# Last two groups of pass 1 joined in a seven-product scheme, first loads split, and a new order of matmuls in pass 2

## What is computed

```python
base = jnp.einsum('bsi,oi->bso', x, W)                       # W 512 x 512
low = jnp.einsum('bsi,bir->bsr', x, lora_A[labeler_index])   # rank 32, 5 labels
delta = jnp.einsum('bsr,or->bso', low, lora_B_w) * 0.5
x = x + base + delta
```

```python
K = 2.0 * jnp.einsum('hn,hnl->hl', Ct, jnp.exp(P)).real      # 32 heads x 512 taps
y = irfft(rfft(x, n=1024) * rfft(K, n=1024)[None])[..., :512] + x * D[:, None]
x = x + y * (arange(512) < length)[:, None, :]
```

## Time and profile before

| | us |
|---|---|
| three timed runs | 192.64, 192.66, 196.02; median 192.66 |
| the profiled execution, its own time | 192.58 |
| its span, first to last instruction | 190.9 |
| TensorE busy | 185.6 (97%) |
| VectorE, ScalarE, GpSimd busy | 125.9, 91.3, 68.7 |
| group 5 of pass 1 with the taps | about 81.4 to 97.5 |
| groups 6 and 7 | about 97.5 to 126.6 |
| pass 2 | about 126.6 to 187.9 |

### The profile page before, as it was taken

The page is one execution under the profiler, slowest core; times in us unless marked ns, Lnnn a source line. Parts: engine busy times, 40 slices in busy tenths (PEclk is TensorE's granted clock), DMA queues, the critical chain, the costliest instruction groups (busy, mean ns, idle before and its releaser), DMA issues.

```text
span 190.9 us, 2653 instructions
## 1 busy us (share of the span) xinstructions
PE 185.6 (97%) x933; PEld 156.6 (82%) x933; DVE 125.9 (66%) x164; ACT 91.3 (48%) x144; POOL 68.7 (36%) x111
## 2 busy tenths in 40 slices
PE   7799999999999999999999999999999999999994
PEld 2487887888888888888888888888999999999993
DVE  0599979458977048858607407279987777786743
ACT  2456066254148754154463312766565656565600
POOL 6038840000000268100000000379886666676600
PEclk9999999999999999999999999999999999999999
DMA  6999990000000000000001600045988788897433
GB/s 191 349 366 422 424 408 11 0 0 2 3 2 0 0 2 3 0 0 0 0 3 34 200 0 0 0 146 167 309 285 295 282 261 291 277 274 270 181 139 138
DMA packets 14797, 27.35 MB, mean 143 GB/s; under 512 B 2592, under 2 KB 5056, under 8 KB 13888
## 3 DMA queue, kind: packets, MB, share of 16 engines
q1 hardware_dynamic: 14064, 25.81, 39.1%
q10 hardware_dynamic: 720, 1.38, 2.1%
HBM read 18.71 MB, written 8.47 MB: 142 GB/s over the span
## 4 chain that ended last, share of the span: by engine, by line
PE 95%; DVE 2%; ACT 1%; issue 0%
PE y_ps L553 13%; PE y_ps L554 12%; PE y_ps L555 12%; PE k_ps L620 10%; PE k_ps L621 10%; PE k_ps L622 10%; PE low_ps L547 4%; PE low_ps L549 4%; PE low_ps L548 4%; PE y_ps L560 4%; PE y_ps L569 2%; PE y_ps L573 2%; PE y_ps L577 2%; PE low_ps L526 2%; PE k_ps L536 1%; PE k_ps L555 1%
## 5 line engine op out<-in xcount | busy, mean ns | idle before, releaser
L406 POOL TENSOR_TENSOR t_lo<-w_raw,t_hi 128x512 fp32r<-128x512 f32 x32 | 44.3, 1393 | 38.0 <-ACT t_hi L468 37.8
L620 PE MATMUL k_ps<-xs_hi,t_hi 128*128 128x128 f32 (+3 forms) x130 | 41.5, 319 | 0.2 <-DVE x_all L829 0.2
L621 PE MATMUL k_ps<-xs_hi,t_lo 128*128 128x128 f32 (+3 forms) x130 | 41.5, 319 | 0.0
L622 PE MATMUL k_ps<-xs_lo,t_hi 128*128 128x128 f32 (+3 forms) x130 | 41.4, 318 | 0.0
L553 PE MATMUL y_ps<-x_hi,w_hi 128*128 128x512 f32 x104 | 40.6, 391 | 0.0
L555 PE MATMUL y_ps<-x_lo,w_hi 128*128 128x512 f32 x104 | 40.6, 391 | 0.0
L554 PE MATMUL y_ps<-x_hi,w_lo 128*128 128x512 f32 x104 | 40.6, 390 | 0.0
L757 DVE COPY_PREDICATED low_sel<-lab_mask,low_ps 32x512 f32<-32x512 int32 x32 | 23.3, 729 | 25.0 <-PE low_ps L549 24.1
L829 DVE COPY_PREDICATED x_all<-len_mask,k_ps 128x512 f32<-128x512 int32 x31 | 23.3, 750 | 13.1 <-PE k_ps L622 13.0
L769 DVE TENSOR_TENSOR xs_lo<-x_all,xs_hi 128x512 fp32r<-128x512 f32 x32 | 28.1, 883 | 4.6 <-ACT xs_hi L462 4.6
L462 ACT CAST xs_hi<-x_all 128x512 fp32r<-128x512 f32 x32 | 19.9, 622 | 19.7 <-PE k_ps L622 19.7
(11 more groups left out here) (132 smaller groups left out, 221.4 us busy)
## 6 DMA issues: line engine op xcount, KB each, us to landing
w_raw<-k_pad SPq DMA_DIRECT2D x32, 256.0 KB, 4.2
out<-x_all SPq DMA_DIRECT2D x31, 256.0 KB, 3.3
x_all<-in_xt SPq DMA_DIRECT2D x7, 1024.0 KB, 12.3
w_raw<-in_wt ACTq DMA_DIRECT2D x4, 256.0 KB, 5.4
x_all<-in_xt SPq DMA_DIRECT2D x4, 256.0 KB, 7.2
ab_raw<-in_ab SPq DMA_DIRECT2D x1, 320.0 KB, 3.7
...
```

The source lines that it names most:

```text
L406: g.tensor_tensor(t_lo[:, k % TR, :], t_raw[:, k % RAW, ::-1], f32(t_hi[:, k % TR, :]), ALU.subtract).then_inc(t_lo_done, 1)
L620: mm(o, t_hi[:, u, cols(lag)], xs_hi[:, b, x], start=(lag == 0), stop=False, skip_group_check=True)
L621: mm(o, t_lo[:, u, cols(lag)], xs_hi[:, b, x], start=False, stop=False, skip_group_check=True)
L622: return mm(o, t_hi[:, u, cols(lag)], xs_lo[:, b, x], start=False, stop=ends, skip_group_check=True)
```

## The change

**Groups 6 and 7 together** (`PAIR` = 6). The two groups' x (8 heads) and W are seen as 2 x 2 blocks, and the four block products with their sums are made with seven products instead of eight (Strassen's scheme in its form with fifteen sums). GpSimd makes the four sums of W's quarters (in place in `w_raw`) and four of the x quarters (in place in `x_all`) after `k_gains`, and then three `_lo` parts of the W sums; ACT and DVE split the seven x operands; the remaining seven sums are taken on DVE and ACT when products leave PSUM (`mix`, DVE; `alpha_read`, ACT). The low-rank part of group 7 is made from the sum of A's halves, and one B difference is needed. Each product is 12 matmuls of 512 columns.

**The first loads.** `ab_raw` comes in two transfers, its first 32 rows first, and the cast of the first `x_hi` moves from ACT to DVE.

**Pass 2.** In `pass2` the three lag-3 matmuls (128 columns) no longer stand together at the head's end, but one behind each of the three lag-0 matmuls (512 columns). The empty table `BETWEEN` and its code are gone. SBUF buffers are laid out anew; `t_raw` loads wait for the last W sum's `_lo`.

On POOL, after `k_gains`:

```diff
+            pool.wait_ge(w_hi_done, CH + 1)
+            pool.wait_ge(w_lo_done, CH)
...
+            g.tensor_tensor(w22, w21, w22, ALU.add).then_inc(s_sum, 1)
+            pool.wait_ge(s_sum, 1)
+            g.tensor_tensor(w21, w21, w11, ALU.subtract).then_inc(s_sum, 1)
+            pool.wait_ge(s_sum, 2)
+            g.tensor_tensor(w11, w22, w11, ALU.subtract).then_inc(s_sum, 1)
+            pool.wait_ge(s_sum, 3)
+            g.tensor_tensor(w12, w12, w11, ALU.subtract).then_inc(s_sum, 1)
...
+            pool.wait_ge(x_load[PAIR], 16)
+            pool.wait_ge(op_lo_done, op_at["X11"])
+            g.tensor_tensor(x11, x12, x11, ALU.subtract).then_inc(x_sum, 1)
+            pool.wait_ge(x_sum, sum_at["T1"])
+            g.tensor_tensor(x12, x12, x22, ALU.subtract).then_inc(x_sum, 1)
+            pool.wait_ge(x_sum, sum_at["T3"])
+            pool.wait_ge(op_lo_done, op_at["X22"])
+            g.tensor_tensor(x22, x22, x11, ALU.subtract).then_inc(x_sum, 1)
+            pool.wait_ge(x_sum, sum_at["T2"])
+            pool.wait_ge(op_lo_done, op_at["X21"])
+            g.tensor_tensor(x21, x21, x22, ALU.subtract).then_inc(x_sum, 1)
```

On ACT, in the loop over g, ahead of `stack_low(g)`:

```diff
+                if g == ACT_KGEN:
+                    act.wait_ge(x_load[PAIR - 1], 16)
+                    split_op_hi("X11")
+                    act.wait_ge(x_load[PAIR], 16)
+                    split_op_hi("X22")
...
+                if g == PAIR - 1:
+
+                    act.wait_ge(x_used, PAIR - 1)
+                    act.wait_ge(x_sum, sum_at["T3"])
+                    split_op_hi("T3")
+                    act.wait_ge(x_sum, sum_at["T2"])
+                    split_op_hi("T2")
```

On DVE, in the loop over g and behind it:

```diff
                 if g == DVE_KGEN:
                     k_reciprocal()
+                    split_op_lo("X11")
+                    split_op_lo("X22")
                 if g == DVE_KGEN + 1:
                     k_scale()
+                    split_op_lo("X21")
...
+                if g == PAIR - 1:
+                    split_op_lo("T3")
+                    split_op_lo("T2")
+
+            split_op_lo("T4")
+            split_op_lo("T1")
+            select_low(PAIR)
+            select_low(PAIR + 1)
+
+            def mix(d, o, i, bank, m):
+                dve.wait_ge(m_done, m_at[m] + d + 1)
+                v.tensor_tensor(o, i, bank[d].rearrange("p (h b) -> p h b", b=P), ALU.add).then_inc(mixed, 1)
```

On PE, a product, and the third of the seven, behind group 5, both groups' low-rank rows and two products:

```diff
+            def product(o, d, wh, wl, name, start):
+
+                for c in range(2):
+                    last = three(by_head(o[d]), wh[:, c, cols(d)], wl[:, c, cols(d)], name, c, start and c == 0, False)
+                return last
...
+            wait_op("T1")
+            for d in range(2):
+                pe.wait_ge(y_read, CH * (PAIR - 1) + d + 3)
+                product(gamma, d, s_hi[:, 0, :, :], s_lo[:, 0, :, :], "T1", True)
+                if d == 0:
+                    wait_low(PAIR + 1)
+                plus_b(gamma, d, b_stack[:, cols(2 + d)], PAIR + 1).then_inc(m_done, 1)
```

On PE, a head of pass 2:

```diff
             def pass2(h):
                 wait_head(h)
-                for lag in range(CH):
-                    last = blocks(y2_ps[h % 2][:, lag * P:L], h, lag, lag, CH - lag, lag == CH - 1)
+                o, b, u = y2_ps[h % 2], h % XR, h % TR
+                near, far = cols(0), cols(CH - 1)
+
+                for t, x in ((t_hi, xs_hi), (t_lo, xs_hi), (t_hi, xs_lo)):
+                    mm(o, t[:, u, near], x[:, b, :], start=(t is t_hi and x is xs_hi), stop=False, skip_group_check=True)
+                    mm(o[:, far], t[:, u, far], x[:, b, near], start=False, stop=False, skip_group_check=True)
+                for lag in (1, 2):
+                    last = blocks(o[:, lag * P:L], h, lag, lag, CH - lag, lag == 2)
                 last.then_inc(y2_done, 1)
```

At the start, on SP and DVE:

```diff
-            sp.dma_start(ab_raw[:], ab).then_inc(ab_load, 16)
+            sp.dma_start(ab_raw[0:RANK, :], ab[0:RANK, :]).then_inc(ab_load[0], 16)
+            sp.dma_start(ab_raw[RANK:P, :], ab[RANK:P, :]).then_inc(ab_load[1], 16)
...
+                    if n == 1:
+                        dve.wait_ge(x0_load[0], 16)
+                        v.tensor_copy(x_hi[:, 0:GH, cols(0)], x_all[:, 0:GH, cols(0)]).then_inc(x0_hi_done, 1)
```

More of the change, by code:

```diff
@@ L38 @@
 MASK_GROUP = 5
-BETWEEN = {}
+PAIR = GROUPS - 2
 ROUND = 1.5 * 2.0 ** 23
@@ L473, in ahead, with split_op_hi @@
                     split_xs_hi(h + LEAD)
-            first = min(BETWEEN, default=GROUPS - 1)
-            for g in range(GROUPS):
+            def split_op_hi(name):
+                s.copy(hi_of[name], raw_of[name]).then_inc(op_hi_done, 1)
+            for g in range(PAIR):
                 if g == 0:
@@ new lines, in _ @@
+            for c in range(CH):
+                last = three(o, a_hi[:, c, :], a_lo[:, c, :], ("X11", "X21")[c // 2], c % 2, c == 0, c == CH - 1)
+            last.then_inc(low_done, 1)
+            wait_op("T3")
+            pe.wait_ge(a_sum_hi_done, 1)
+            pe.wait_ge(a_sum_lo_done, 1)
+            pe.wait_ge(low_read, (NLAB - 1) * PAIR)
+            o = by_head(low_ps[:, (PAIR + 1) % 2, :])
+            for c in range(2):
+                three(o, a_sum_hi[:, c, :], a_sum_lo[:, c, :], "X22", c, c == 0, False)
@@ new lines, in _ @@
+            for c in range(2):
+                last = three(o, a_hi[:, c, :], a_lo[:, c, :], "T3", c, False, c == 1)
+            last.then_inc(low_done, 1)
+            pe.wait_ge(k_copied, 1)
+            for d in range(2):
+                product(alpha, d, w11, w11_lo, "X11", True).then_inc(m_done, 1)
+            wait_op("T2")
+            pe.wait_ge(s_hi_done, 3)
+            pe.wait_ge(s_lo_done, 3)
+            for d in range(2):
+                pe.wait_ge(y_read, CH * (PAIR - 1) + d + 1)
+                product(beta, d, s_hi[:, 1, :, :], s_lo[:, 1, :, :], "T2", True).then_inc(m_done, 1)
@@ new lines, in _ @@
+            for d in range(2):
+                pe.wait_ge(alpha_read, d + 1)
+                product(alpha, d, w12, w12_lo, "X21", False)
+                plus_b(alpha, d, b_stack[:, cols(d)], PAIR).then_inc(m_done, 1)
+            pe.wait_ge(s_hi_done, 4)
+            pe.wait_ge(s_lo_done, 4)
+            pe.wait_ge(b_diff_hi_done, 1)
+            pe.wait_ge(b_diff_lo_done, 1)
+            for d in range(2):
+                pe.wait_ge(mixed, mixed_at["C22"] + d + 1)
+                product(gamma, d, s4, s4_lo, "X22", False)
+                plus_b(gamma, d, b_diff[:, cols(d)], PAIR + 1).then_inc(m_done, 1)
@@ L681, in _ @@
+            for d in range(2):
+                pe.wait_ge(mixed, mixed_at["U3"] + d + 1)
+                product(beta, d, w22, w22_lo, "T4", False)
+                plus_b(beta, d, b_stack[:, cols(2 + d)], PAIR).then_inc(m_done, 1)
+            for h in range(LAST):
+                if h < 2:
+                    pe.wait_ge(alpha_read, 3 + h)
                 pass2(h)
```

260 lines of the change are left out of this document (196 added, 64 removed).

## The result

The changed kernel takes 206.52 us (median of 5, 203.30 to 206.68) against 192.64 for the kernel before, measured beside it. By the ratio it takes 1.061 times as long, 95% interval 1.056 to 1.066. In all ratios here executions over 1.5% above the fastest of their kernel count as slow and are left out, while the medians have them in: this ratio rests on 203.30 and 205.56, 204.4 in the mean. That is slower by more than 2%, as forecast, and 4.5 us more than the forecast of 202.0 by the median, 2.4 by the two executions of the ratio.

The account below looks back on a forecast made before the run. TensorE's stream was taken to bound the kernel, busy 185.6 of 190.9 us. The terms, 192.6 - 1.7 - 0.3 + 0 + 9.2 + 2.0 + 0.4, gave 202.2, stated as 202, with a range of 192 to 207.

Parts of the forecast that it names:

- Fewer matmuls: Groups 6 and 7: 116 matmuls in place of 128, taking 2.7 us out.
- The wait inside the seven products: Third product's group 7 low-rank matmul: TensorE waits 0.9 to 1.0 us for a 13.2 us chain against 12.3 of cover.
- The hiccup before the third head: Change of pass: 0.2 us idle and a late weight load before the third head go, counted as 0.3 us saved.
- The short matmuls: Pass 2: loads start only one matmul ahead, so the new order saves 0, bounds 0 and -5.1 us.
- Rival 1: Pass 2: the short matmuls' loads do hide, the wait comes as forecast; 197.1 us, chance 0.12.
- GpSimd's sums and who waits for them: Group 5: GpSimd and VectorE take turns, delaying casts and label selection; TensorE waits 8.5 to 9.9 us, taken as 9.2.
- Rivals 2 and 3: Group 5: engines take no turns, 193.7 us, chance 0.08; GpSimd's plain sums are cheap, 191.0 us, chance 0.05.
- The clock: Behind group 5's wait: idle time drops TensorE to half speed for some microseconds, +2.0 us, bounds 0 and 3.2.
- The start: First loads up to group 1: VectorE's added cast and sums run late, +0.4 us, bounds -0.3 and +1.0.
- the narrower 198.5 to 206: Whole kernel: the forecast case's own range, with the wait between 7 and 10.5 us and the clock between 0 and 3.2.

Follow-up runs that it names:

- the last kernel: Changed kernel with the old start and the moved sums and splits set where VectorE selects labels or idles: 190.98 us, ratio 0.991.
- both kernels on it: Old order of pass 2 matmuls put into the changed kernel: 204.77 us, 1.063; new order alone in the kernel before: 192.50 us, 0.9993.
- the kernel with the gap filled: Changed kernel with 38 unused 512-column matmuls added in TensorE's group 5 wait: 202.26 us, ratio 1.051.

## Why the prediction was right, and where it was off

1. *Fewer matmuls, -2.7.* Right: busy time 185.6 to 182.9 in the last kernel, where the clock stays up.
2. *The wait inside the seven products, +1.0.* The mechanism was right, the term was undersized: 1.61. By the rows, the chain from the pair's start to the second stacking took 125.72 - 111.65 = 14.07, not 13.2. Label selection, stacking and difference together take 4.6 a group here, not 4.3, since each hand-over between VectorE and ScalarE adds 0.1 to 0.2 to the busy times that I had added up; the rest is in the cast and difference ahead. The pair so brought 0.8 and not 1.7. Of the 0.9 missing, 0.6 is this wait; the rest lies in no wait that the profile names: without it the 116 matmuls stand 0.231 apart, where the 128 of the kernel before stand 0.228 apart (29.24), and why stays open.
3. *The hiccup before the third head, -0.3.* Right: 143.90 - 140.10 = 3.80 for two heads, where the earlier trace rows give 130.71 - 126.57 = 4.14. The other 0.3 of the table's last line were not forecast; they lie behind the third head, mostly in the last stores.
4. *The short matmuls, 0.* Right, by both kernels on it: 192.50 with the new order alone, heads 1.90 apart. The reading of the weight-load rows, one matmul ahead and no more, held. Rival 1 falls.
5. *GpSimd's sums and who waits for them, +9.2.* Right in size (9.02) and in its parts. `k_gains` took 82.21 - 71.00 = 11.2 from the chain's start, where the earlier trace rows have 9.7: 1.5 later, with 1.6 forecast, and 1.8 came back when the two differences were moved. The sums took 1.6 (the first 2.2) and 2.7 to 3.2. The forecast restart, 98.1 to 99.5, becomes 101.1 to 102.5 with the 3.0 of the start; it was 101.70. That VectorE's label selection holds TensorE without ScalarE's casts was shown twice, by moving the casts (wait 8.8) and by summing T2 nine microseconds earlier (6.1); that ScalarE's casts would hold it alone is read from the rows. With the sums and the X11 and X22 splits moved, the wait is gone. Rivals 2 and 3, no turn-taking and cheap sums, fall.
6. *The clock, +2.0.* Right: 2.1 by the count of matmuls, 2.0 by the kernel with the gap filled. The mechanism held, half speed for some microseconds behind the gap. The size was in part luck: it was picked between 0 and 3.2 from the warm-up matmuls, during which the profile of the kernel before reads a granted clock of 1.00 although they stand 0.45 apart, so that those rows did not show how long a fallen clock stays down.
7. *The start, +0.4, bounds -0.3 and +1.0.* This step failed: it cost 3.0. I had weighed VectorE's extra 1.3 against a slack of 0.6, and wrote "the earlier first 32 rows of `ab_raw` may give back some tenths; the transfers behind it come one issue later". The cast of the first x chunk that moved to VectorE did little or nothing (203.02 with it, 202.34 without). The split transfer did the harm: the x chunk behind it was used at 8.59 and not near 6.2, TensorE's first product started 1.2 later (9.07 against 7.88), and from 10.5 to about 13.5 the granted clock was 0.50, so that the first twelve matmuls took 4.7 us (9.07 to 13.79) instead of 2.8. What brings the clock down there is not shown: it is not the length of this wait alone (see the last section). Splitting alone costs the kernel before 0.8 to 5 us. The forecast counted the issue of one more transfer, not what it does to the arrival of those behind it, and nothing in my bounds allowed for that.

In the profiled execution, 205.56, the terms account for the difference from the forecast of 202.2: 2.6 at the start, 0.9 in the pair, less 0.2 in group 5's wait and 0.3 in pass 2, and some tenths of rounding. The median is a microsecond higher still, within the scatter of this kernel; its executions were not traced but for this one. The range, 192 to 207, held, but 206.52 lies above the narrower 198.5 to 206. Those two bounds also do not follow from their terms: a wait of 7 with no fall of the clock gives 198.0, and 10.5 with 3.2 gives 204.7.
